# Selective scan of layer 0 with B, C and dB held in PSUM, and 38 units of the neighbouring gather beside it

## What is computed

```
xd = einsum('bdl,kd->blk', x, xw)                   # the rows dt, B (16) and C (16)
delta = softplus(einsum('blr,dr->bld', dts, dtw) + dtb)
dA = exp(delta[..., None] * A)                      # A: 16 states for each channel
dBx = delta[..., None] * Bs[:, :, None, :] * xt[..., None]
def step(h, inp):
    da, dbx, c = inp
    h = h * da + dbx
    return (h, einsum('bdn,bn->bd', h, c))
y = ys + xt * Dv                                    # then a layer norm
```

```
samp = (v00 * (1 - wx) + v01 * wx) * (1 - wy) + (v10 * (1 - wx) + v11 * wx) * wy
return einsum('hwpc,hwp->hwc', samp, m)             # 9 samples, 16 groups of 32 channels
```

## Time and profile before

| what | value |
|---|---|
| time, median of 3 runs | 15028.0 us (15008.2 to 15036.4) |
| the profiled execution: time, span | 14996.4 us, 14994.6 us |
| busy share of the span: PE, DVE, ACT, POOL | 54%, 67%, 22%, 72% |
| instructions of DVE and POOL | 9944 and 9221 |
| mean granted PE clock | 0.757 |

### The profile page before, as it was taken

One profiled execution on the slowest core, in us unless ns is written; L12 is line 12 of the kernel. 1 busy time (PEld: TensorE's weight loads), 2 busy tenths in 40 slices (PEclk: granted clock), 3 DMA queues, 4 the chain that ended last, 5 costly groups with the idle time before them and its releaser, 6 DMA issues. The chain is left out here.

```text
span 14994.6 us, 97001 instructions
## 1 busy us (share of the span) xinstructions
PE 8042.7 (54%) x31008; PEld 3924.1 (26%) x31008; DVE 10011.0 (67%) x9944; ACT 3295.1 (22%) x4747; POOL 10724.0 (72%) x9221
## 2 busy tenths in 40 slices
PE   5671457545575456564575456655575555750005
PEld 3240214222242223222242222323232222420002
DVE  6753886669675796658766696757866697753333
ACT  3330223112220233112231132202321122310000
POOL 0007887778777887778877787778877787777771
PEclk8885679777788678786788678886787767885558
DMA  1012111321132212321123211321124211232111
GB/s 66 9 34 70 38 49 53 103 71 35 55 82 74 65 36 60 101 77 36 51 63 92 70 36 56 90 87 42 38 60 104 72 36 53 70 85 59 54 54 45
DMA packets 890427, 913.01 MB, mean 61 GB/s; under 512 B 692417, under 2 KB 702657, under 8 KB 880642
## 3 DMA queue, kind: packets, MB, share of 16 engines
q0 software_dynamic: 294912, 604.57, 14.2%
q1 hardware_dynamic: 594946, 301.65, 7.0%
HBM read 770.26 MB, written 135.28 MB: 60 GB/s over the span
## 5 line engine op out<-in xcount | busy, mean ns | idle before, releaser
L124 POOL DMA_INDIRECT gat<-corner_tables,idx x9216 | 10723.5, 1164 | 3984.3 <-issue 2790.3
L138 DVE TENSOR_TENSOR gat<-gat,wts 128x1152 f32<-128x1152 f32 x1024 | 1388.9, 1356 | 2602.7 <-DMA gat<-corner_tables,idx 2472.5
L763 PE MATMUL PS<-hc,ident 128*128 128x512 f32 (+2 forms) x4096 | 1974.7, 643 | 1611.4 <-DVE hc L819 1563.0
L142 DVE TENSOR_REDUCE dcn<-gat 128x32 f32<-128x1152 f32 x1024 | 2159.0, 2108 | 38.8
L763 PEld LDWEIGHTS PS<-hc,ident 128*128 128x128 f32 x4096 | 935.9, 271 | 2467.0 <-DVE hc L819 1987.9
L854 DVE TENSOR_TENSOR_SCAN hs<-dA,dB 128x1024 f32<-128x1024 f32 (+2 forms) x672 | 1535.9, 2287 | 28.9 <-issue 19.3
L1061 PE MATMUL PS<-ident,E 128*128 128x128 f32 x4096 | 601.1, 294 | 454.8 <-ACT ET L1130 257.3
L819 DVE TENSOR_TENSOR hc<-hs,Cs 128x1024 f32<-128x1024 f32 x672 | 805.6, 1199 | 42.5 <-PE PS L763 42.5
L1140 ACT ACTIVATE E<-PS,nmax 128x1024 f32<-128x1024 f32 x512 | 570.5, 1114 | 1000.3 <-DVE nmax L1195 785.8
L779 ACT ACTIVATE Cs<-PS 128x1024 f32<-128x1024 f32 x296 | 303.0, 1024 | 2184.9 <-DVE hc L819 2184.9
L1719 PE MATMUL PS<-M,wp 128*32 128x512 f32 x5120 | 618.1, 626 | 163.9 <-DVE wp L1772 92.1
(11 more groups left out here) (252 smaller groups left out, 11239.7 us busy)
## 6 DMA issues: line engine op xcount, KB each, us to landing
gat<-corner_tables,idx POOLq DMA_INDIRECT x9216
corner_tables<-xp SPq DMA_DIRECT2D x1024, 64.0 KB, 2.2
D<-in_dist_dram SPq DMA_DIRECT2D x8, 4096.0 KB, 14.4
wqkv<-in_qkv_w_dram SPq DMA_DIRECT2D x8, 3072.0 KB, 11.6
corner_tables<-gat SPq DMA_DIRECT2D x1, 17280.0 KB, 54.9
X<-in_x_dram SPq DMA_DIRECT2D x32, 512.0 KB, 5.2
w_in<-in_in_w_dram SPq DMA_DIRECT2D x16, 1024.0 KB, 6.2
w_c<-in_c_w_dram SPq DMA_DIRECT2D x16, 1024.0 KB
```

The costliest lines, as they stand in the source:

```text
L124: nc.gpsimd.indirect_dma_start(bd.gat[n % NG][:, k * 4 * CG:(k + 1) * 4 * CG], None, bd.rows, bass.IndirectOffsetOnAxis(ap=bd.idx[:, m, g ...
L138: nc.vector.tensor_tensor(v, v, wv, ALU.mult).then_inc(self.prod, 1)
L142: nc.vector.tensor_reduce(bd.dcn[m % 2][:, g * CG:(g + 1) * CG], gat[:].rearrange("p (k c) -> p c k", c=CG), AX.X, ALU.add).then_inc(self. ...
L763: mm = nc.tensor.matmul(PS[:, p.ybank(t, d, h), 0:p.hl], self.ident[:], src[:, j, h * p.hl:(h + 1) * p.hl], start=(c == 0 and j == 0), sto ...
```

## The change

In the scan, the rows B and C stay in PSUM, where PE puts them, and are broadcast anew for each tile instead of each chunk. `dB` is made in place in PSUM. Each channel half goes through all of its chunks before the other begins, so that the sums of one half need two banks instead of four. ACT's copies are gone. `dA` has no gap columns: the position that is first in the direction of a run gets a decay of zero instead, so that ACT makes `dA` for each run and not for each tile, into one of four buffers. The `SHARE` of the scan goes from 30 to 38 units, that of six other stages down by nine in all: 127 of 128 units then have a stage, and the last is done by the wait for the whole gather at prepare's end, which both kernels have.

```diff
-                dA = [self.sb(c2, f"dA{i}", [P, SEG]) for i in range(3)]
-                dB = [self.sb(c2, f"dB{i}", [P, SEG]) for i in range(2)]
-                Bs = [self.sb(c2, f"Bs{i}", [P, N]) for i in range(2)]
-                Cs = [self.sb(c2, f"Cs{i}", [P, N]) for i in range(2)]
+                dA = [self.sb(c2, f"dA{i}", [P, N]) for i in range(4)]
...
+        dB = [flat(PS[:, 2 + 2 * i:4 + 2 * i, :]) for i in range(2)]
+        Cb = flat(PS[:, 6:8, :])
...
+                broadcast(0, 0, 2, b_done)
+                broadcast(0, 1, 6, c_done)
+                broadcast(1, 0, 4, b_done)
+                for u, (k, n, p, t, c, d) in enumerate(runs):
+                    final = u + 1 == tile_runs[k]
+                    if final and k + 2 < len(tiles):
+                        pe.wait_ge(scanned, u + 1)
+                        broadcast(k + 2, 0, 2 + 2 * (k % 2), b_done)
                     pe.wait_ge(hc_ready, u + 1)
+                    if final and k + 1 < len(tiles):
+                        broadcast(k + 1, 1, 6, c_done)
+                    if c == 0 and n:
+                        pe.wait_ge(y_kept, 2 * n)
...
-                        nc.scalar.activation(dst[ci % 2][:].rearrange("p (i f) -> p i f", i=2),
-                                             PS[:, 2 * which:2 * which + 2, :], ACT.Copy).then_inc(bc_out, 1)
...
+                for u, (k, n, p, t, c, d) in enumerate(runs):
+                    if u >= 4:
+                        act.wait_ge(scanned, u - 3)
+                    z, inner = p.shaped(dA[u % 4]), p.inner(d)
+                    if p.nn > 1 and u - pass_starts[p.tag] < 4:
+                        nc.scalar.activation(z[:, :, p.first(d)],
+                                             self.ones[:, 0:p.nn].rearrange("p (n a) -> p n a", a=1), ACT.Copy, scale=0.0)
...
-                    nc.vector.tensor_tensor(p.body(dB[k % 2]), p.shaped(Bs[ci % 2]), src, ALU.mult)\
-                        .then_inc(weighed, 1)
+                    z = p.shaped(dB[k % 2])
+                    nc.vector.tensor_tensor(z, z, src, ALU.mult).then_inc(weighed, 1)
...
-                    nc.vector.tensor_tensor(p.body(hc[u % 2]), p.body(hs[u % 2]), p.shaped(Cs[ci % 2]), ALU.mult)\
-                        .then_inc(hc_ready, 1)
+                    nc.vector.tensor_tensor(hc[u % 2][:], hs[u % 2][:], Cb, ALU.mult).then_inc(hc_ready, 1)
...
+                    a_, b_, h_ = dA[u % 4][:], dB[k % 2], hs[u % 2][:]
                     if p.dirs[d] < 0:
                         a_, b_, h_ = (z[:, ::-1] for z in (a_, b_, h_))
                     nc.vector.tensor_tensor_scan(h_, a_, b_, 0.0, ALU.mult, ALU.add).then_inc(scanned, 1)
                     if u:
                         multiply(u - 1)
-                    if c == 0 and t == 1 and d == 0 and p is not passes[0]:
-                        keep(passes[passes.index(p) - 1])
+                    if n and u == part_runs[n - 1] + 1:
+                        keep(n - 1)
+                    if d == 0 and k + 1 < len(tiles):
+                        weigh(k + 1)
                     spread()
...
-SHARE = {"finish": 4, "norm3": 1, "gram": 7, "power": 12, "norm0": 3, "conv": 6, "steps": 9, "scan": 30, "norms": 6,
-         "out": 2, "norm1": 2, "attention": 32, "norm2": 1, "prepare": 13}
+SHARE = {"finish": 4, "norm3": 1, "gram": 7, "power": 12, "norm0": 2, "conv": 5, "steps": 8, "scan": 38, "norms": 5,
+         "out": 2, "norm1": 1, "attention": 28, "norm2": 1, "prepare": 13}
```

More of the change, by code:

```diff
@@ L229, in __init__ @@
         self.chunks = NS // self.nn
[L230 to L239, removed]
     def shaped(self, z):
@@ L751, in _, with broadcast @@
-                broadcast(0)
-                broadcast(1)
-                for u, (k, ci, p, c, t, d) in enumerate(runs):
-                    if t == 0 and d == 0 and ci + 2 < len(chunks):
-                        broadcast(ci + 2)
-                    pe.wait_ge(hc_ready, u + 1)
-                    if c == 0 and p is not passes[0]:
-                        pe.wait_ge(y_kept, kept_by[passes[passes.index(p) - 1].tag])
-                    src = p.body(hc[u % 2])
+                def broadcast(k, which, bank, done):
+                    n, p, t, c = tiles[k]
+                    per = max(1, NH // p.L)
+                    for i in range(2):
+                        for j in range(per):
+                            row = which * NS + c * p.nn + (i * per + j if p.nn > 1 else 0)
+                            pos = slice(0, p.L) if p.nn > 1 else slice(i * NH, (i + 1) * NH)
+                            mm = nc.tensor.matmul(PS[:, bank + i, j * p.hl:(j + 1) * p.hl],
+                                                  self.pick[:, row:row + 1].to_broadcast([3 * BC, P]),
+                                                  p.bc[:, pos], start=True, stop=True)
+                    mm.then_inc(done, 1)
@@ L782, in _ @@
-                copies(0)
-                for k, (ci, p, c, t) in enumerate(tiles):
-                    if k >= 3:
-                        act.wait_ge(scanned, last_run["tile", k - 3])
-                    if c == 0 and t == 0 and p is not passes[0]:
-                        act.wait_ge(gaps_zero, len(dA + dB) * len([x for x in passes[:passes.index(p)] if x.nn > 1]))
+                for u, (k, n, p, t, c, d) in enumerate(runs):
[5 more added lines that the diff above has]
+                                             self.ones[:, 0:p.nn].rearrange("p (n a) -> p n a", a=1), ACT.Copy, scale=0.0)
@@ new lines, in keep @@
+                def keep(n):
+                    p, t = parts[n]
+                    dve.wait_ge(y_done, part_runs[n])
+                    for d in range(len(p.dirs)):
+                        for h in range(p.halves):
+                            sl = slice(h * p.hl, (h + 1) * p.hl)
+                            nc.vector.scalar_tensor_tensor(
+                                out=p.y[d][:, t, sl], in0=p.f[:, t, sl], scalar=self.col(f"Dv{p.wi}", t),
+                                in1=PS[:, p.ybank(d, h), 0:p.hl], op0=ALU.mult, op1=ALU.add)\
+                                .then_inc(y_kept, 1)
@@ L848, in _ @@
+                weigh(0)
+                for u, (k, n, p, t, c, d) in enumerate(runs):
+                    dve.wait_ge(da_ready, u + 1)
                     dve.wait_ge(weighed, k + 1)
```

115 lines of the change are left out of this document (35 added, 80 removed).

## The result

| | before | after |
|---|---|---|
| median | 15031.19 us (15008.22 to 15036.38, 4 runs) | 14511.27 us (14510.16 to 14513.36, 4 runs) |
| ratio | | 0.9657, 95% interval 0.9640 to 0.9674 |
| span of the profiled execution | 14994.6 us | 14508.8 us |

The kernel is 520 us faster. The prediction had 14200 us, 14000 to 14480: the direction was right, the gain was over-estimated by some 310 us, and the time lies 31 us above the range. In thirteen of the later runs the kernel before, run beside them, itself took 17.66 to 17.88 ms in place of 15.02; such times are given with that one's, and compared with it alone.

The account below looks back on a forecast made before the run. POOL's indirect DMAs were taken to pace all stages. An image falls from 1742 to 1624 us, seven times -118 is -826; with +10 for the head, 14996.4 becomes 14180, plus 20 gives 14200 us, range 14000 to 14480.

Parts of the forecast that it names:

- All 242 scan instructions of an image lose their second SBUF input: Scan on DVE: POOL's indirect DMAs are no longer held up, saving POOL 175 us an image.
- norms to prepare: Last stretch of an image, including attention: 691 us before, forecast 603 us with less waiting for the gather.
- finish to steps: First stretch of an image, still paced by POOL: three units fewer, 529 us before, forecast 496 us.
- PSUM costs DVE nothing: Scan instructions on DVE: no change from PSUM inputs, bounds 0 to +24 us an image.
- The last rival: Scan: the recurrence out of PSUM is itself slower; if its time doubled, 15720 us; chance 0.04.
- PE hides behind DVE ... Cost nothing; bounds 0 to 1 us x 64.: Scan's one-direction runs: PE's summing and broadcasting adds nothing to DVE's time, bounds 0 to 1 us for each of 64.
- if DVE waits for PE before L796: Scan: sign that the prediction is wrong, DVE waiting for PE before the multiplication with C; no size given.
- the head: First image's part, before POOL gets its first addresses: forecast 10 us longer, from +13 and -3.
- PE or PSUM latency enters DVE's chain: Scan rival: up to 1 us for each of 64 runs in eight scans, about +500, 14450 to 14700 us; chance 0.08.
- my 525: Scan stretch of an image, bound by DVE's chain: 490 plus 27.6 for eight units plus 7 exposed waits, 525 us.
- Shares that fit better: Whole-loop rival: POOL's 1567 us an image is the bound, up to -175 x 7, 13780 us; chance 0.05.
- its own case: Whole program, the prediction's main forecast: 14200 us, range 14030 to 14370, chance 0.70.

Follow-up runs that it names:

- the fitted shares: The changed kernel with B broadcast one run earlier, plus SHARE finish 3, norm0 1, conv 4, steps 6, scan 41, attention 30, prepare 14: 14320.03 us, ratio 0.9535.

## Why the prediction was right in part and wrong in size

**Right: POOL was the bound, and two SBUF inputs on DVE are what held it up.** "All 242 scan instructions of an image lose their second SBUF input": a DMA in the scan went to 1001 ns, where 950 to 1000 was forecast. The relief is 142 us an image and not 175. With the old shares it is 164 (1149.9 / 7), at 969 ns in the scan; with the new shares a DMA is a little longer in every stretch (1.00 us in the scan, 1.11 in norms to prepare and 1.10 in finish to steps, against 0.97, 1.08 and 1.08 with the old). Why, no run shows; the gather's units, whose L135 has two SBUF inputs too, stand closer there. This was not what limited the scan: POOL stood for 57.1 us in it, where "some 30" was forecast. One reading was off without harm: the DMA that begins at 3614.23 ends 0.75 us after the recurrence and not about with it, as the one beside dB ends 0.82 us after dB.

**Right: PSUM costs DVE nothing.** Recurrence 2281 ns (2285 in the kernel before with new shares), multiplication 1195 (1197), dB 1226 to 1228 (1212 to 1215 in the one-direction passes): 1 us an image, where 0 to 24 were kept open. The last rival, a slower recurrence, is out.

**Right: finish to steps.** 496 forecast, 497 measured.

**Wrong: "PE hides behind DVE ... Cost nothing; bounds 0 to 1 us x 64."** I compared sums of work (5.67 us of PE against 6.2 of DVE), priced the one-direction runs alone, and looked for the wait at the multiplication, for C; the sign of being wrong, "if DVE waits for PE before L796", stood at that place too, and that wait is 0. PE works in the order of its list: C, which has to wait for the multiplication, then 3.62 us of sums, and B last, though B's banks had been free since the recurrence's end. So B comes up to 0.8 us too late in 22 of the 64 one-direction tiles, in the example where PE was at 1.2 GHz and no gather unit stood between, and up to 4.8 us too late where 16 states lie side by side and PE sums for 7.06 us, more than DVE's 4.7 for a run. The granted clock over the scan is 0.74, lower than 0.83 in the head before; in the head's scan after, at 0.81, only one of the 64 waits, for 0.61 us. The price is shown by the experiment that moves B and nothing else: 167 us, 22 for each of seven images and 7 in the head (of 219.6 us of waits in eight scans). The rival "PE or PSUM latency enters DVE's chain" had a chance of 0.08. Its mechanism is what happened, at 22 us an image and not at 64, at dB and not at the multiplication. With B moved, the scan takes 518.5 us against my 525.

**Mis-sized: norms to prepare.** 621 us for 603. For attention I added 23 for its chain without gather and 14 for the units: 335. It took 345: without units it is 328 now and not 321, and the units add 17. Two groups of DVE in the stretch from norms to prepare:

```profile
L135 DVE TENSOR_TENSOR gat<-gat,wts 128x1152 f32<-128x1152 f32 x51 | 68.9, 1351 | 4.5 <-DMA gat<-corner_tables,idx 4.1 <-PEq L182 0.4
...
L1154 DVE TENSOR_TENSOR kk<-PS,cols 128x512 f32<-128x512 f32 x8 | 5.5, 691 | 37.5 <-PE PS L1002 37.5
```

The waits for the gather are down from 112.3 to 4.1, and what DVE waits for now is PE, at attention's start and between its steps: it is attention's own chain with 28 units laid in it. The 328 is the first image's, with none, where it was 321, at a granted clock of 0.95 against 0.97; that makes 7 of the 10, and why the clock is lower no run shows. The other 8 us of the 18 lie behind attention, in prepare and at the barrier after it. These are readings, with no experiment made for them.

**Mis-sized: the base and the head.** One image stood for seven: 1742 us, where the mean, from one list of addresses to the next, is 1732 (seven in 12124.5 us). In the kernel after the image read is 1662 and the mean 1659, so some 7 us of each image's gain, 46 in all, never were there. And the head is 27 us longer, not 10 (1135.0 against 1108.6): its scan 18 us, from 392 to 410, most of the rest attention.

The sum: an image took 38 us more than forecast (scan 19, norms to prepare 18, finish to steps 1), 38 x 7 = 266, and with 46 and 17 that is 329, for the 330 us between the 14180 forecast for the profiled execution and its 14510. B's late broadcast is 167 of them; without it the scan would be 6.5 us shorter than forecast.

**The chances.** "Shares that fit better" (0.05) presumed that POOL's need is the floor. It isn't: once POOL is relieved, each stretch has a chain of its own near its present length, and moving units about by hand gave at most 24 us. Two sums of the prediction are slightly off, without weight for the forecast: halfway between 13780 and its own case is 13980 and not 13950, and the cases that it names as faster add up to 0.93 before any part of the last rival, not to 0.92.

## What to carry to other kernels

When a shared resource is relieved, cost the next bound not by sums of work but by each in-order engine's own list: for each item of it ask since when it could have run, and what stands before it. Here the order of two items on PE was worth 167 us, on top of a gain of 520. An operand moved to PSUM can speed up a program through GpSimd without making VectorE a nanosecond faster, but the work that GpSimd can then do has to be scheduled to that place, else (-248 us for -520) half of the gain is lost.

## What the runs showed of the hardware

- Of DVE's three kinds of instruction in the scan, the recurrence alone, at 2.29 us with two SBUF inputs, costs POOL 749 us in 588 of them beside a gather, 1.27 us each. A DMA that begins inside such a recurrence ends 0.75 to 0.76 us after it (1.83 us long, in the kernel before and in the run with dB in SBUF). With one input in PSUM, POOL's DMA beside it takes 0.95 us.
- A PSUM input costs none of the three kinds more than 16 ns of 1.2 to 2.3 us. The Trainium skill (VectorE: DVE Perf Modes, section "The TRN2 errata") gives a fixed part of 58 cycles for an SBUF source and of 120 for a PSUM source. No row here shows such a difference; the measurement decides.
- Where the kernel before took 17.66 to 17.88 ms, the head was as long as ever: with the fitted shares POOL waited 1121.0 us for the first list of addresses (run of 17171 us), against 1130.8 in the run of 14320 us. But in the whole program the trace holds long waits, for some of which it names no releaser but "remote":

```profile
POOL gat L121 <- DVE dcn L139: 3299.1, 512, 56.8
...
DVE ET L1178 <- remote: 839.3, 83, 20.8
...
ACT row L1718 <- remote: 691.2, 55, 33.9
```

POOL there waits for DVE to free a buffer for 3299.1 us, against 572.4 for the same kernel in the run of 14320 us, whose trace has no remote releaser among its 200 largest waits. What holds these operations no run shows; the cause is open.
